# One attention layer with a mixture of experts behind it: routing in three parts, another order of the attention step, and all shared tiles ahead of the routed ones

## What is computed

```python
def attention(x):                       # 16 heads of 64, one key and value head
    xn = ln(x, g_norm)
    q = (xn @ Wq).reshape(b, n, 16, 64).transpose(0, 2, 1, 3)
    k, v = split(xn @ Wkv)              # with one null key and value ahead
    sim = einsum('bhid,bjd->bhij', l2norm(q) * q_scale, l2norm(k) * k_scale) * 8
    attn = softmax(causal(sim + bias))  # keys 129 = 128 and the null key
    return ln(einsum('bhij,bjd->bhid', attn, v) @ Wout, g_out)

def ffn(x):                             # x: the attention's result
    out = expert(x, shared)             # silu(x @ g.T) * (x @ u.T) @ d, width 352
    w = normalised softmax weights of the 2 best of 7 experts of each token
    return out + sum(w[..., e] * expert(x, routed[e]) for e in range(7))
```

## Time and profile before

| | us |
|---|---|
| median of 3 runs (433.98, 434.51, 672.77) | 434.51 |
| the profiled execution | 434.13 |
| its span, first to last instruction | 432.0 |
| PE busy in the span | 357.3 (83%) |
| DVE / ACT / POOL busy | 292.6 / 279.5 / 229.2 |
| mean granted TensorE clock | 0.929 |

### The profile page before, as it was taken

How to read it: one execution, slowest core, us unless ns; L and a number is a source line. 1 busy time by engine, 2 the same in 40 slices (tenths; PEclk the granted TensorE clock), 3 DMA queues, 4 the chain that set the end, 5 groups by cost and what they waited for, 6 DMA issues and landing times.

```text
span 432.0 us, 10178 instructions
## 1 busy us (share of the span) xinstructions
PE 357.3 (83%) x2921; PEld 295.1 (68%) x2922; DVE 292.6 (68%) x1144; ACT 279.5 (65%) x935; POOL 229.2 (53%) x253
## 2 busy tenths in 40 slices
PE   0286776999999999999998989697619999999980
PEld 0275655677777777777776648496519999999980
DVE  1848385888888888888889894757305565566545
ACT  1385594999999999999996773464304444444440
POOL 5024843678876667667872552277730444344420
PEclk9998995999999999999999687869958999999997
DMA  6726299990000000000000000011121222111117
GB/s 185 204 80 200 67 212 191 202 163 2 2 2 2 3 2 2 3 0 2 3 2 2 1 2 0 14 50 58 49 56 26 63 61 61 49 56 55 35 58 236
DMA packets 39479, 26.55 MB, mean 61 GB/s; under 512 B 4464, under 2 KB 37130, under 8 KB 39438
## 3 DMA queue, kind: packets, MB, share of 16 engines
q1 hardware_dynamic: 34256, 20.60, 21.8%
q0 software_dynamic: 2240, 4.23, 2.9%
q10 hardware_dynamic: 2942, 1.21, 1.1%
HBM read 12.89 MB, written 13.54 MB: 61 GB/s over the span
## 4 chain that ended last, share of the span: by engine, by line
PE 60%; DVE 16%; POOL 7%; issue 7%; ACT 5%; DMA 4%; SPq 1%; ACTq 0%; DVEq 0%; POOLq 0%
PE bank L1188 45%; PE bank L1185 14%; POOL sent_rows L537 7%; DVE p_space L1014 2%; ACT p_space L687 2%; DMA q_space<-in_L_cond_g_dram 2%; DVE biasm_space L1140 1%; DVE xn L934 1%; DMA bias<-result_rows 1%; DVE low L1018 1%; DVE p_space L841 1%; ACT xn L610 1%; DVE GL L918 1%; ACT yh L779 1%; DVE norm_in L812 1%
## 5 line engine op out<-in xcount | busy, mean ns | idle before, releaser
L687 ACT ACTIVATE p_space<-p_space,low 128x129 f32<-128x129 f32 x256 | 99.0, 391 | 6.4 <-DVE low L1018 6.4
L502 POOL TENSOR_TENSOR p_space<-p_space,inv 128x516 f32<-128x516 f32 x64 | 67.1, 1049 | 66.1 <-DVE inv L1026 66.1
L1014 DVE SCALAR_TENSOR_TENSOR p_space<-bank,rn,biasm_space 128x129 f32<-128x129 f32 x256 | 72.0, 343 | 22.3 <-PE bank L1188 22.0
L493 POOL TENSOR_TENSOR biasm_space<-bias,madd 128x516 f32<-128x516 f32 x64 | 75.6, 1192 | 7.4 <-DVE p_space L1014 7.3
L543 POOL DMA_INDIRECT result_rows<-oT_space,dest_ring x38 | 37.6, 990 | 60.8 <-DVE dest_ring L1154 60.1
L768 ACT ACTIVATE biasm_space<-bank 128x384 f32<-128x384 f32 x54 | 26.6, 492 | 58.1 <-PE bank L1185 58.0
L1185 PE MATMUL bank<-ident,p_space 128*128 128x128 f32 (+1 forms) x272 | 48.5, 297 | 2.4 <-POOL p_space L502 2.1
L687 ACT ACTIVATION_READ_ACCUMULATOR p_space<-p_space,low 128x1 f32 x256 | 48.5, 190 | 0.0
L1188 PE MATMUL bank<-DT,biasm_space 128*128 (+1 forms) x324 | 46.4, 281 | 1.2 <-ACT biasm_space L768 1.2
L702 ACT ACTIVATE pT<-bank 128x512 f32<-128x512 f32 x64 | 37.3, 583 | 13.9 <-PE bank L1188 12.8
L1018 DVE TENSOR_REDUCE low<-p_space 128x4 f32<-128x516 f32 x64 | 44.2, 691 | 2.2
(11 more groups left out here) (217 smaller groups left out, 705.4 us busy)
## 6 DMA issues: line engine op xcount, KB each, us to landing
sent_rows<-fill_row SPq DMA_DIRECT2D x2, 1950.0 KB, 24.1
sent_rows<-fill_row SPq DMA_DIRECT2D x2, 1885.0 KB, 19.6
q_space<-sent_rows SPq DMA_DIRECT2D x38, 65.0 KB, 1.9
xs<-in_x_dram SPq DMA_DIRECT2D x4, 256.0 KB, 6.3
bias<-bias_rows SPq DMA_DIRECT2D x1, 1024.0 KB, 5.8
xn<-result_rows SPq DMA_DIRECT2D x4, 256.0 KB, 4.4
bias<-result_rows SPq DMA_DIRECT2D x4, 256.0 KB, 5.6
out_dram<-xs SPq DMA_DIRECT2D x4, 256.0 KB, 2.5
```

The costliest lines, as they stand in the source:

```text
L493: nc.gpsimd.tensor_tensor(biasm[:, b % 2, heads, :], bias[:, heads, :], madd[:, b:b + 1, :].to_broadcast([P, HC, KEYS]), ALU.add).then_inc ...
L502: nc.gpsimd.tensor_tensor(v, v, spread(inv[:, b % 2, heads], KEYS), ALU.mult).then_inc(p_normed, 1)
L687: last = nc.scalar.activation(v, v, ACT.Exp, bias=low[:, b % 2, h:h + 1], accum_out=den[:, b % 2, h:h + 1])
L1014: last = nc.vector.scalar_tensor_tensor(Pb[:, q, h, :], src, rn[:, q, h:h + 1], biasm[:, q, h, :], ALU.mult, ALU.add)
```

## The change

It makes three parts (8, 4 and 4 batches), with buffers and pads for three; part 0 is chosen in step 17, part 1 in steps 17 and 18, part 2 between the first tiles. The step's order differs on all four engines; half of `keep_oT` goes from ACT to DVE; `null_out` and `pnT` get 128 rows, of which 112 are zero. `AHEAD` is 16. The diff, cut to its core (left out: buffers and banks of the three parts, counts of semaphores, the split of `oT_kept` in two). The indentation is shortened.

```diff
-    Y_FIRST = NB - 4
-    PARTS = (range(0, Y_FIRST), range(Y_FIRST, NB))
+    PARTS = (range(0, NB - 8), range(NB - 8, NB - 4), range(NB - 4, NB))
...
     CHAIN = 11
-    CONSTS = 23
+    CONSTS = 25
     MLP0_DMAS, MLP_DMAS, ROW_DMAS, SCALE_DMAS, EXPERT_DMAS = 3, 5, 3, 5, 5
...
     RING = 4
-    AHEAD = 12
+    AHEAD = 16
     LAPS = (ROUTED - RING) // RING
...
-null_out = sb("null_out", [H, D])
+null_out = sb("null_out", [P, D])
...
-pnT = sb("pnT", [H, P])
+pnT = sb("pnT", [P, P])
...
-y_bank = (3, 1, 2, 6)
+y_bank = (4, 4, 2, 6)
...
         norm_p(2, 3)
-        add_mask(2, 2)
+        norm_p(3, 3)
+        norm_p(0, 2)
         add_mask(0, 0)
-        norm_p(3, 3)
-        add_mask(3, 2)
-        norm_p(0, 2)
+        norm_p(1, 2)
+        add_mask(3, 1)
+        add_mask(2, 0)
         add_mask(1, 0)
-        norm_p(1, 2)
...
+    def stage(k, m):
+        act.wait_ge(biasm_first, 2 * NB)
+        act.wait_ge(biasm_made, 2 * NB)
+        act.wait_ge(y_normed, PARTS[k].stop // 4)
+        nc.scalar.activation(send[k][m][:, :, 0:D], y_sb[:, PARTS[k].start:PARTS[k].stop, :],
+                             ACT.Copy).then_inc(send_made[k][m], 1)
...
-        def keep_oT(g, back):
+        def keep_oT():
+            if on(3):
...
         if t == NB + 2:
-            weigh(0)
+            weigh(1)
         keep_q(0)
...
         square_q(0)
-        keep_oT(1, 3)
+        keep_oT()
         if t != NB + 1:
...
             keep_across(act, LATE[1])
+        keep_q(1)
         keep_pT(1)
-        keep_q(1)
         square_q(1)
...
             keep_up(act, LATE[2])
+        if t == NB:
+            keep_yT(0)
         if t == NB + 1:
-            for g in range(Y_FIRST // 4):
-                keep_yT(g)
+            stage(0, 1)
+            keep_yT(2)
         keep_pT(2)
+        if t == NB + 1:
+            weigh(0)
         exp(1, 1)
+        if t == NB:
+            keep_yT(1)
         keep_sums()
...
             keep_across(act, LATE[2 * t])
-        keep_oT(0, 2)
+        keep_pn()
         keep_pT(3)
-        keep_pn()
         if t == 0:
...
-    act.wait_ge(biasm_first, 2 * NB)
-    act.wait_ge(biasm_made, 2 * NB)
-    act.wait_ge(y_normed, Y_FIRST // 4)
-    nc.scalar.activation(send[0][1][:, :, 0:D], y_sb[:, 0:Y_FIRST, :], ACT.Copy).then_inc(send_made[0][1], 1)
+    for m in range(TOP):
+        stage(1, m)
...
+        def keep_oT():
+            if on(2):
+                b = t - 2
+                dve.wait_ge(mixed, NCH * b + 2)
+                need(dve, y_made, b - 1)
+                nc.vector.tensor_copy(oT[:, p, 0:HALF * P].rearrange("p (k s) -> p k s", k=HALF),
+                                      bank[6][:, :].rearrange("p (k s) -> p k s", k=HALF)[:, :, ::-1]).then_inc(oT0_kept, 1)
         def invert(c, back):
...
         scores(0)
+        if t == NB:
+            dve.wait_ge(router_turned, 1)
+            nc.vector.tensor_scalar(router_wT[:, 0:NE], bank[4][:, 0:NE], gocol[:, 0:1], None, ALU.mult).then_inc(router_kept, 1)
+        invert(3, 2)
         scores(1)
-        invert(3, 2)
         if t == 0:
...
         if t == NB + 1:
-            dve.wait_ge(router_turned, 1)
-            nc.vector.tensor_scalar(router_wT[:, 0:NE], bank[2][:, 0:NE], gocol[:, 0:1], None, ALU.mult).then_inc(router_kept, 1)
-        if t == NB + 2:
             choose(0)
...
             share_out(0)
+        if t == NB + 2:
+            rank(1)
+            share_out(1)
         keep_y()
+        if t == NB + 1:
+            choose(1)
+            mark(1)
         if t > 1:
...
             invert(0, 1)
+        keep_oT()
         scores(3)
...
         invert(2, 1)
+        if t == NB - 3:
+            root_y(0)
         if t == NB - 2:
-            gather_y(Y_FIRST - 1)
-            root_y(0)
+            scale_y(0)
+            scale_y(1)
         if t == NB - 1:
-            scale_y(0)
+            root_y(1)
         if t == NB:
-            scale_y(1)
             scale_y(2)
...
             gather_y(NB - 1)
-            root_y(1)
+            root_y(2)
             scale_y(3)
         if u == 2:
-            choose(1)
+            choose(2)
         if u == 3:
-            mark(1)
-            rank(1)
-            share_out(1)
+            mark(2)
+            rank(2)
+            share_out(2)
         if u == 5:
-            list_tiles(0)
+            list_tiles()
...
         pe.wait_ge(y_normed, g + 1)
-        pe.wait_ge(biased, NCH * NB)
-        if g == Y_FIRST // 4 - 1:
+        if y_bank[g] == 4:
             pe.wait_ge(router_kept, 1)
+            need(pe, yT_kept, g)
+        else:
+            pe.wait_ge(biased, NCH * NB)
         for b in range(4 * g, 4 * g + 4):
...
     def logits(g):
-        pe.wait_ge(router_kept, 1)
+        k = max(k for k in range(len(PARTS)) if 4 * g >= PARTS[k].start)
+        pe.wait_ge(biased, NCH * NB)
         pe.wait_ge(yT_kept, g + 1)
         for b in range(4 * g, 4 * g + 4):
-            last = mm(bank[logit_bank(b)][:, b * NE:(b + 1) * NE], YT[:, b * P:(b + 1) * P], router_wT[:, 0:NE], True, True)
-        if 4 * g + 4 in (Y_FIRST, NB):
+            last = mm(logits_at(k)[:, b, :], YT[:, b * P:(b + 1) * P], router_wT[:, 0:NE], True, True)
+        if 4 * g + 4 == PARTS[k].stop:
             last.then_inc(logits_made, 1)
...
+        if t == NB + 1:
+            logits(0)
+            logits(1)
         if t == NB + 2:
-            count(0)
+            count(1)
         queries(0)
         turn_p(0)
+        mix(2, 3)
         mix(3, 3)
+        if t == NB:
+            pe.wait_ge(q_squared, 2 * NB)
+            pe.wait_ge(pn_kept, NB - 2)
+            turn(bank[4][:, 0:NE], router_sb[:, :]).then_inc(router_turned, 1)
         scores(0, 1)
...
             expert_up(LATE[2 * t])
+        if t == NB:
+            turn_y(0)
         if t == NB + 1:
-            pe.wait_ge(biased, NCH * NB)
-            turn(bank[2][:, 0:NE], router_sb[:, :]).then_inc(router_turned, 1)
-            for g in range(Y_FIRST // 4):
-                turn_y(g)
+            turn_y(2)
         project()
         if t == NB + 1:
-            for g in range(Y_FIRST // 4):
-                logits(g)
+            count(0)
+            logits(2)
         turn_p(2)
...
         scores(2, 1)
+        scores(3, 1)
         mix(1, 2)
+        if t == NB:
+            turn_y(1)
         sum_squares()
...
             expert_across(LATE[2])
+        turn_pn()
         turn_p(3)
-        scores(3, 1)
         turn_sums()
...
             expert_across(LATE[3])
-        turn_pn()
-        mix(2, 2)
```

More of the change, by code:

```diff
@@ L169, in rows_in_tile @@
             return tile[:, :, :].rearrange("p a b -> p (a b)")[:, 0:n * ROW].rearrange("p (b c) -> p b c", c=ROW)
-        send = ((rows_in_tile(bias, Y_FIRST), rows_in_tile(madd, Y_FIRST)),
-                (shared(p_space, 0, NB - Y_FIRST, ROW), shared(p_space, (NB - Y_FIRST) * ROW, NB - Y_FIRST, ROW)))
+        send = tuple(tuple(rows_in_tile(tile, PARTS[1].stop)[:, PARTS[k].start:PARTS[k].stop, :] for tile in (bias, madd))
+                     for k in range(2)) + (
+                tuple(shared(p_space, m * len(PARTS[2]) * ROW, len(PARTS[2]), ROW) for m in range(TOP)),)
         whole = (shared(p_space, H * KEYS + (NB + 1) * DH, 2, I), shared(biasm_space, (NB + 1) * 2 * DH, 2, I))
@@ L205, in adaln_ffn_kernel, with run_end @@
         placed = shared(o_space, 7 * NB * NE, TOP, NB, NE)
-        run_up = (shared(o_space, 9 * NB * NE, 2, PADS[0] + Y_FIRST, NE), shared(o_space, 12 * NB * NE, 2, PADS[1] + NB - Y_FIRST, NE))
+        RUNS = [2 * (PADS[k] + len(PARTS[k])) * NE for k in range(len(PARTS))]
+        run_up = tuple(shared(o_space, 9 * NB * NE + sum(RUNS[0:k]), 2, PADS[k] + len(PARTS[k]), NE) for k in range(len(PARTS)))
+        assert sum(RUNS) <= 4 * NB * NE
+        def run_end(k):
+            return run_up[k][:, SIDES[k], PADS[k] + len(PARTS[k]) - 1, :]
         tiles_up = shared(o_space, 13 * NB * NE, 2, EPAD + NE)
@@ L649, in _ @@
             act.wait_ge(null_turned, 1)
[L650 removed]
+            nc.scalar.activation(null_out[0:H, :], bank[7][0:H, 0:D], ACT.Copy).then_inc(null_kept, 1)
             def keep_yT(g):
@@ L787, in between @@
                 if u == 1:
-                    keep_yT(Y_FIRST // 4)
+                    keep_yT(3)
                 if u == 2:
                     for m in range(TOP):
-                        nc.scalar.activation(send[1][m][:, :, 0:D], y_sb[:, Y_FIRST:NB, :], ACT.Copy).then_inc(send_made[1][m], 1)
+                        stage(2, m)
                 if u == 3:
-                    weigh(1)
+                    weigh(2)
             run_tiles(act, step, between)
@@ L940, in choose @@
                 lb, eb = L[:, b, :], equal[:, b, :]
-                own(nc.vector.tensor_tensor(lb, bank[logit_bank(b.start)][:, 0:NB * NE].rearrange("p (b e) -> p b e", b=NB)[:, b, :],
+                own(nc.vector.tensor_tensor(lb, logits_at(k)[:, b, :],
```

(4 more changed lines are left out.)

76 lines of the change are left out of this document (40 added, 36 removed).

## The result

The changed kernel takes **449.56 us** (median of 4 runs, 448.66 to 451.28) against 434.25 us for the kernel before in the same job (median of 4): a ratio of 1.036, 95% interval 1.032 to 1.040. One of those four executions, of 672.77 us, was a slow one and is left out of the ratio. The change makes the kernel slower. The profiled execution has a span of 446.6 us, 14.6 longer than before.

The account below looks back on a forecast made before the run. DVE with POOL was taken as the new bound, at 12.9 us a step. Start +6.3, steps 3 to 12 +8.4, steps 13 to 15 +3.5 and routing and tiles -5.0 made +13.2 on 434.13: 447 us, range 424 to 456.

Parts of the forecast that it names:

- The held links: Attention step: POOL's masks hold two links of DVE's chain of norms, making a step 12.9 us instead of 12.06.
- the first rival: Attention step: links pass between POOL's instructions, or masks wait; PE's 11.5 us step decides, 420 us in all; chance 0.17.
- the second: Rival: one mask meets the chain and expert loads hide the start; step 12.0, 432 us in all; chance 0.13.
- PE's own step: Attention step on PE: matmuls of 128 rows and paired scores and mixes cut its need from 12.06 to 11.5 to 11.6 us.
- The start: Until step 3: seven masks in a row at first, then held links in steps 1 and 2, add 6.3 us.
- the reasoning of the step: Part of the start: the attention step's argument about masks holding links, taken to add 2.1 us in each of steps 1 and 2.
- Steps 13 to 15: Last three steps before routing: held links plus roots and scalings behind them make 46.4 us instead of 42.9, +3.5.
- first scatter at 20 to 25, I take 23: Routing: POOL's first row scatter comes 23 us after step 16's start, 5.5 earlier than in the kernel before.
- the first shared tile starts some 32 after: PE behind the steps: first shared tile some 32 us after step 16's start, against 28.6 in the kernel before.
- The warm first tile: Routed tiles: PE comes warm to the first one, which takes 2.4 us instead of 4.0, -1.6.
- no shared ones between its halves: Last routed tile: two shared tiles of some 0.9 us no longer stand between its halves, -1.8.
- The third rival: Attention steps: PE also falls to the half clock in its new waits; one us on ten steps gives 457; chance 0.10.

Follow-up runs that it names:

- E1: Kernel after, with POOL's order in the attention step put back to that of the kernel before; 426.94 us, ratio 0.988.
- E5: Kernel before, with only POOL's new order in the attention step taken from the change; 452.15 us, ratio 1.049.
- E10: Kernel after, with one of its three late masks (mask 3) moved ahead of scaling 3 on POOL; 439.05 us, ratio 1.012.
- E11: Kernel after, with each mask's addition on POOL replaced by two memsets, mask and bias left out of the computation; 422.70 us, one execution.
- E13: E7 with one DVE instruction, the scaling of the router's weights, moved from step 16 to the end of step 15; 419.01 us, ratio 0.967.
- E12: E1 with the second part's choice, count, exponential, ranks and shares all moved later; 424.66 us, ratio 0.979.
- E4: Kernel after, with twelve shared tiles ahead of the routed ones instead of sixteen; 447.22 us, ratio 1.030.
- E7: E1 with twelve shared tiles ahead of the routed ones instead of sixteen; 422.32 us, ratio 0.973.

## Why the prediction was right, and where it was off

The forecast, 447 in 424 to 456 and most likely slower, held: 449.56. Point by point:

- **The held links** are shown, not only argued: E1 takes them away, E5 brings them into the kernel before, E10 takes one of two, E11 makes POOL write only. So the first rival (the links pass) and the second (half the loss) fell: two holds a step, and +5.8 at the start. The step was 12.76 instead of 12.9. The masks beside the chain ended 11.0 after the step's start, as forecast; it was the third and fourth links that they held (202.17 and 203.32), the second having just passed. The added copy took 0.66 for 0.70. One reading was wrong and changed nothing: of the held instructions of the earlier trace rows, which "agree" by their two inputs, the one at 230.05 (L929) reads a single tile.
- **PE's own step** was mis-sized: "11.5 to 11.6" is 11.10 in E1. Counted from each start on PE to the next, a step of E1 is shorter than one of before by 0.31 on the turns of P, 0.20 on the scores, 0.19 on the null matmuls, 0.15 on the mixes and 0.09 on the projection. I had 0.2, 0.2 and 0.1 for the middle three, near enough, and nothing for the turns and the projection. It didn't enter the sum, as DVE was the bound. The first rival's step was too long by 0.4 for this reason. E1 is the case with that rival's free chain.
- **The start** came to +5.8 for +6.3, and E1 gives all of it back. Its parts were 1.5, 1.7 and 2.6, where I had 2.0, 2.1 and 2.1 (which make 6.2); "the reasoning of the step" gives 1.7 (12.9 for 11.2), not 2.1, so the sum came near partly by luck. **Steps 13 to 15** came to +2.6 for +3.5. In E1, without masks beside the norms, they take 44.7, so 1.8 of the 2.6 are there still: the roots and scalings that now stand behind these steps. They aren't free of POOL either: in E1 two links of each of the two roots are held (207.16, 208.25, 236.64 and 237.73, 1.05 to 1.11 each).
- **The step that failed** is "first scatter at 20 to 25, I take 23", with "the first shared tile starts some 32 after": they were 26.7 and 37.4. My working of step 16 had DVE's chunks, the copy and one exponential, and choosing from 11.1 on. Choosing began at 15.9. I had overlooked that the turn of y on PE now waits for the router's scaled weights, which stand on DVE behind a root and a chunk; the projection is queued behind that wait and then runs at the half clock, and DVE waits 3.20 for it. E13 takes this wait away, and the first scatter comes at 23.2, the first shared tile 3.0 earlier. The second part's count I had named, but took for less than its wait of 3.69. E12, where that part's routing stands later, has the first shared tile at 32.2, 5.3 earlier than E1, though most of that is lost again at the tiles. No run has both moves, so how the 5.4 by which this tile came late divide between the two stays open. The sixteen tiles took 38.1 for 39.6, so the stage came to +2.4 instead of -1.6.
- **From the first routed tile on**, -3.4 was forecast and measured, but only half of it for the reason given. The warm first tile gave 1.85 for 1.6. The other term, -1.8 for "no shared ones between its halves", isn't there: from the start of the last routed tile to the last scatter of a result it takes 9.36 instead of 9.43, and E13, with four shared tiles in that place, takes 106.80 from the first routed tile on, against 106.60. What made up for it lies elsewhere: 0.5 in the tiles between, and 1.0 from that last scatter to the end (15.78, where the trace of before has 16.82 and the others 15.5 to 16.3). That is luck. E4 and E7 add what I hadn't weighed: with twelve tiles ahead the first routed tile runs at the half clock again, but the routed tiles start earlier, and that is worth more.
- **The third rival** (PE at the half clock in the steps) fell: PE idles 1.42 a step and the granted clock is 1.00 in all of 91.10 to 218.97.

The terms that missed have opposite signs: the three stages of steps were forecast 2.6 too dear, the routing 4.0 too cheap. That 447 lies so near 449.56 is partly this, and so partly luck.

## What to carry to other kernels

Before an instruction of GpSimd is moved to fill idle time, look at what DVE does in that time: a chain of small dependent instructions with two SBUF inputs paid here for each mask beside it, up to 0.94 us for a link of 0.17. Idle time on one engine that lines up with such a chain on another was the schedule's cover, not waste. And of a new wait on PE, look at what stands ahead of its releaser in the other queue: in E13 one instruction's place moved the first scatter by 3.5 us.

## What the runs showed that was not expected

PE kept the full clock through 1.42 us of waiting in every step of 12.76, for 128 us; in the stage with its waits of 4.90 and 3.69 the granted clock was 0.73. A held link ends some 0.03 us behind the mask beside it (204.44, the mask at 204.40), whenever it started: one that starts in the last 0.15 us of a mask (201.95, the mask ending at about 202.1) takes 0.18 and loses nothing, one that starts 0.3 ahead of the end takes 0.35 (E5, 181.97), the next ones 1.11. So how much a chain loses turns on a few tenths: E5 has 0.35, 1.11 and 1.11 where the kernel after has 0.18, 1.11 and 1.12. And two inputs in SBUF aren't the only case: besides the one at 230.05, a scaling of the results (L958) is held, 1.07 instead of 0.32 for the second of the five from 247.64 in the kernel after, beside a POOL scaling, and it reads a single tile and scalars. E11 doesn't tell of those.
